# Second cross attention of a two-layer Perceiver block: four PSUM banks for scores, one for the mix, and steps of 3, 3, 3, 2, 2 tiles on TensorE

## What is computed

```
def _L1_xattn_ref(x, context, mask, Wq, Wkv, Wout, b_out):
    HEADS, DIM_HEAD = 16, 64
    q = x @ Wq.T
    k, v = split(context @ Wkv.T, 2, axis=-1)      # 16 heads each
    sim = einsum('bhid,bhjd->bhij', q, k) * DIM_HEAD ** -0.5
    sim = where(mask[:, None, None, :], sim, max_neg)
    attn = softmax(sim, axis=-1)
    out = einsum('bhij,bhjd->bhid', attn, v)       # heads merged
    return out @ Wout.T + b_out
```

## Time and profile before

| | us |
|---|---|
| median of 3 runs | 3442.48 |
| lowest and highest run | 3437.34, 3446.69 |
| the profiled execution, its own time | 3440.26 |
| its span in the profile | 3438.4 |
| this stage's tiles, start of the first mix to the last scores | about 1358 to 2846 |
| engine shares of the whole span: PE, DVE, ACT, POOL | 96%, 69%, 56%, 47% |

### The profile page before, as it was taken

How to read it: one execution, slowest core, us unless ns; L and a number is a source line. 1 busy time by engine, 2 the same in 40 slices (tenths; PEclk the granted TensorE clock), 3 DMA queues, 4 the chain that set the end, 5 groups by cost and what they waited for, 6 DMA issues and landing times. The chain is left out here.

```text
span 3438.4 us, 67642 instructions
## 1 busy us (share of the span) xinstructions
PE 3296.8 (96%) x26448; PEld 1900.8 (55%) x26448; DVE 2386.0 (69%) x5437; ACT 1908.8 (56%) x2600; POOL 1611.6 (47%) x1271
## 2 busy tenths in 40 slices
PE   7799999999998998999999999999999998989999
PEld 4566666666655674545544555555554544655555
DVE  7877877877874436777777777777777775653333
ACT  5466666666664234666666666666666663432222
POOL 5433334333322104777777777777777764310000
PEclk7899999999998899999999999999999999989999
DMA  2133333333310002101111011110111001000000
GB/s 75 32 73 78 79 83 74 77 77 77 79 40 1 26 1 74 39 20 39 39 39 39 20 39 39 39 36 23 39 39 39 26 23 50 1 28 4 4 3 4
DMA packets 90541, 138.92 MB, mean 40 GB/s; under 512 B 14512, under 2 KB 67824, under 8 KB 89456
## 3 DMA queue, kind: packets, MB, share of 16 engines
q1 hardware_dynamic: 90224, 134.61, 14.5%
HBM read 94.15 MB, written 1.05 MB: 28 GB/s over the span
## 5 line engine op out<-in xcount | busy, mean ns | idle before, releaser
L2459 ACT ACTIVATE arena<-banks,arena 128x512 f32<-128x512 f32 x832 | 560.5, 687 | 476.6 <-PE banks L2248 476.6
L2273 PE MATMUL banks<-arena 128*128 128x512 f32 x1664 | 803.9, 603 | 0.8 <-ACT arena L2466 0.8
L2207 POOL TENSOR_TENSOR arena<-arena 128x1024 f32<-128x1024 f32 x256 | 604.3, 2360 | 165.5 <-ACT arena L2466 164.3
L1222 DVE TENSOR_REDUCE arena<-banks 128x1 f32<-128x512 f32 (+1 forms) x896 | 529.7, 628 | 155.1 <-PE banks L1055 150.4
L2361 DVE TENSOR_TENSOR banks<-arena,banks 128x512 f32<-128x512 f32 x640 | 444.6, 695 | 242.2 <-ACT arena L2459 222.8
L1359 ACT ACTIVATE arena<-banks 128x1024 f32<-128x1024 f32 (+1 forms) x448 | 424.0, 962 | 272.2 <-PE banks L1136 272.0
L2378 DVE TENSOR_TENSOR arena<-arena,banks 128x1024 f32<-128x1024 f32 (+1 forms) x448 | 507.5, 1134 | 1.6 <-PE banks L2263 1.2
L2466 ACT ACTIVATE arena<-arena 128x1024 f32<-128x1024 f32 (+1 forms) x448 | 443.0, 989 | 11.1 <-DVE arena L2378 10.9
L2273 PEld LDWEIGHTS banks<-arena 128*128 128x128 f32 x1664 | 289.9, 190 | 220.8 <-issue 200.1
L2247 PE MATMUL banks<-arena 128*128 128x512 bf16 x832 | 315.3, 379 | 0.0
L2246 PE MATMUL banks<-arena 128*128 128x512 bf16 x832 | 314.9, 379 | 0.0
(11 more groups left out here) (353 smaller groups left out, 5167.9 us busy)
## 6 DMA issues: line engine op xcount, KB each, us to landing
arena<-arena SPq DMA_DIRECT2D x768, 50.0 KB, 2.2
arena<-in_ctxT SPq DMA_DIRECT2D x32, 800.5 KB, 6.2
arena<-in_ctx SPq DMA_DIRECT2D x32, 768.0 KB
fold<-in_ctxT SPq DMA_DIRECT2D x16, 800.5 KB, 4.6
foldv<-in_ctxT SPq DMA_DIRECT2D x16, 800.5 KB, 4.7
arena<-in_m2w SPq DMA_DIRECT2D x3, 2048.0 KB, 7.9
arena<-in_xw SPq DMA_DIRECT2D x1, 2048.0 KB, 7.9
weights<-in_weights SPq DMA_DIRECT2D x1, 1920.0 KB, 12.2
```

The lines of the kernel that those rows point to most:

```text
L1222: eng.tensor_reduce(o, s, AX, ALU.max).then_inc(a_max, 1)
L2207: eng.tensor_tensor(part, part, tiles, ALU.add).then_inc(sums, 1)
L2273: eng.matmul(c.ps[:, R_MIX + v % 2, :], ctxn[:, b, kt * D:(kt + 1) * D], st[:, v % 2, kt, :], start=kt == 0, stop=kt == KT - 1).then_inc(m ...
L2459: eng.activation(st[:, v % 2, kt, :], c.ps[:, n % SB, :], ACT.Identity, bias=hide[:, kt, v // 2:v // 2 + 1])\
```

## The change

All of it is in `cross_attention_1`. SB becomes 4, so that scores use banks 0 to 3; the banks of the running maximum and of the shift move up by one, and the mix has one bank, 6, in place of two. With one bank, the first mix of unit v waits for `copy_mix(v - 1)` (before: for `copy_mix(v - 2)`). ScalarE issues `copy_mix` ahead of the score copy of kt 0 and no longer behind it. TensorE takes a unit's tiles in five steps of 3, 3, 3, 2 and 2. `between`, and the kt at which each of its entries stands, is unchanged, and so are VectorE's and POOL's programs.

```
-    SB = 3
+    SB = 4
...
-    R_MAX, R_SHIFT, R_MIX, R_SMALL = 3, 4, 5, 7
+    R_MAX, R_SHIFT, R_MIX, R_SMALL = 4, 5, 6, 7
...
             if kt == 0:
                 eng.wait_ge(ctx_loaded[b], (v // 4 + 1) * 32)
-                wait_if(eng, u_made, v - 1)
+                wait_if(eng, u_made, v)
             eng.wait_ge(exps, v * NP + kt // 2 + 1)
-            eng.matmul(c.ps[:, R_MIX + v % 2, :], ctxn[:, b, kt * D:(kt + 1) * D], st[:, v % 2, kt, :],
+            eng.matmul(c.ps[:, R_MIX, :], ctxn[:, b, kt * D:(kt + 1) * D], st[:, v % 2, kt, :],
...
+        steps = [(0, 3), (3, 6), (6, 9), (9, 11), (11, KT)]
         for v in range(UNITS + 1):
-            for j, a, z in tile_pairs:
+            for a, z in steps:
                 tiles = range(v * KT + a, v * KT + z)
...
         def copy_mix(v):
             eng.wait_ge(mixed, (v + 1) * KT)
             wait_if(eng, y_ps, v - 1)
-            eng.activation(u[:, v % 2, :], c.ps[:, R_MIX + v % 2, :], ACT.Copy).then_inc(u_made, 1)
+            eng.activation(u[:, v % 2, :], c.ps[:, R_MIX, :], ACT.Copy).then_inc(u_made, 1)
...
         for n in range(TILES + KT):
             v, kt = n // KT, n % KT
+            if kt == 0 and v > 0:
+                copy_mix(v - 1)
             if n + LEAD < TILES:
                 copy(n + LEAD)
-            if kt == 0 and v > 0:
-                copy_mix(v - 1)
```

More of the change, by code:

```diff
@@ L2303, in final @@
             mm.then_inc(f_ps, 1)
-        stir(c, eng, R_MIX + 1, 14)
+        stir(c, eng, R_MIX, 14)
         eng.wait_ge(hidden, 3)
@@ L2313, in pe @@
             queries(0, x)
-            stir(c, eng, R_MIX + 1, 5)
+            stir(c, eng, R_MIX, 5)
         eng.wait_ge(unit_made, 1)
@@ L2318, in pe @@
             if n == KT + 1:
-                stir(c, eng, R_MIX + 1, 8)
+                stir(c, eng, R_MIX, 8)
                 turn_peaks(0)
         spread_shift(0)
-        stir(c, eng, R_MIX + 1, 10)
+        stir(c, eng, R_MIX, 10)
         def between(n):
```

## The result

The changed kernel takes 3667.07 us (median of 4 runs, 3663.60 to 3674.64) against 3439.91 for the kernel before beside it (4 runs). The ratio is 1.0658, with a 95% interval of 1.0640 to 1.0677. The direction was right. The size was not: the forecast was 3568, with a range that ended at 3603, and 99 us of the 227 us lost were not in it. The profiled execution of after took 3663.60, its span is 3661.7.

The account below looks back on a forecast made before the run. The prediction took TensorE's instruction stream to bound the stage. It added 104 us (projection and turning) and 22 us (query and final) to the profiled 3440.26, giving 3566, or 3568 as a median, with its own range 3558 to 3600.

Parts of the forecast that it names:

- What bounds the kernel: In this stage TensorE is busy throughout, so the time is its instructions' cost, start to start; the change can only add waits.
- Four score banks and fewer steps: On TensorE's scores: a fourth bank removes no wait, and leaving out four score-mix swaps a unit saves zero.
- One mix bank: A unit's first mix waits for the previous unit's copy_mix, with 1.9 us of cover; costed at nothing.
- Projection and turning: Neighbours on bank 7, so the turning waits for VectorE's four steps: 1.68 us more in 61 units, 1.57 in unit 62, 104 us.
- Query and `final`: In units with v % 4 = 2, final directly follows the kt 11 query and waits for q_low: 15 times 1.49, 22 us.
- Does it spread?: After the turning's stall: VectorE needs about 2.6 us before the shift's spread, TensorE has 4.5 us of work; no second wait.
- The range: Forecast's own range 3558 to 3600; 3548 to 3603 takes in the bounds and the mix bank's case, leaving out some 0.15.
- ready work: Rival: TensorE lets mixes past the waiting turning and final, so both stalls go and the time is 3442; chance 0.03.
- swaps were worth nothing: Rival judged: the four f32-bf16 swaps a unit that go were dear, at 0.6 us each giving 3415; chance 0.02.
- The fallen clock: Rival: TensorE, standing 1.8 us in 25, is granted a clock of 0.97, costing 49 us more, 3617; chance 0.06.
- The rule on order: On TensorE weight loads may be pulled ahead but matmuls stay in program order, so the turning's whole stall is lost.

Follow-up runs that it names:

- the banks alone: The changed kernel with TensorE's seven steps back, keeping four score banks, one mix bank and the earlier copy_mix: 3443.01 us, ratio 1.0010 to the kernel before.
- the steps alone: The kernel before with only the five steps of 3, 3, 3, 2, 2, three score banks and two mix banks kept: 3674.90 us, ratio 1.0680.
- the spread moved: The changed kernel with TensorE's spread_shift at kt 9 instead of kt 8: 3562.70 us, ratio 1.0358 to the kernel before.
- a second bank: The changed kernel with its fourth score bank given to the shift, so the spread waits for shifts two units back: 3561.80 us, ratio 1.0337.
- the kernel with idle times of 2.34 us: The kernel before, steps of two, with TensorE's spread_shift at kt 7 instead of kt 8: 3650.74 us, ratio 1.0598.
- the projection by the turning: The kernel before, steps of two, with TensorE's projection at kt 4 instead of kt 3: 3533.22 us, ratio 1.0260.

## Why the prediction was wrong

- **What bounds the kernel**: right. TensorE's instructions did not change in cost; the base unit grew from 22.82 to 26.25 by waits alone.
- **Four score banks and fewer steps at zero**: right, by the banks alone (3443.01), the steps alone with three banks, and equal periods of 95.24 and 95.22 in steps of three and of two.
- **One mix bank at zero**: right. There is no row for it, and the banks alone cost nothing measurable.
- **Projection and turning, 104 us**: right. The stall was 1.80 as worked out. Moving the turning away gave 110 back, 1.76 a unit in the period (103.75 to 96.72): the 1.80 and the further 0.06 of the turning, less 0.10 by which mixes are slower behind the projection. In unit 62, where the scores have run out, the stall was 3.10 us, 1.57 more than the 1.53 of before, as forecast.
- **Query and `final`, 22 us**: right. 15 waits of 1.41; parting them gave 27 (3452.27 to 3425.66), a figure with the error of two medians, and 1.48 a time in the period (96.72 to 95.24), against 1.49.
- **The step that failed** is the sentence "Does it spread?", which ends in "no second wait". It looked at the spread's wait for the halves of the maxima alone, found 4.5 us of cover for 2.6, and stopped. `spread_shift` has a second wait in its next line, `wait_if(eng, shifted, v * NP)`, for the last shift of the unit in hand. In steps of two the spread came a step after the scores that the maxima ahead of that shift wait for; in steps of three, (6, 9) holds both. Measured: 61 waits, 103.3 us in the row, 1.85 a unit start to start, which is 113 us. By the medians it is 104 with the spread moved and 105 with a second bank, and 112 from the steps alone (3674.90) to the spread moved (3562.70), which ran on one chip; the stages ahead vary from execution to execution (the first score starts anywhere from 1325.96 to 1346.75 in the traces here). With this term the sum is 3568 + 61 x 1.85 = 3681 before what is saved elsewhere. After the turning the mixes start cleanly (2106.73 to the next scores in 2.58, where the mixes behind the projection took 0.10 more than 4 x 0.43 in the earlier trace rows), 6 us over the units, which leaves 3675 against 3667. Of the rest, 2.6 are the median of before, 3442.48 when the sum was made and 3439.91 beside the changed kernel. Within the 61 units the terms close: 61 x (1.68 + 1.85 - 0.10) + 15 x 1.49 = 232 against the 231 measured.
- The forecast's test for it was at hand. The trace of before has one wait of L2262 for L2378, 0.6 us, where the stage begins (the first row, from 1358 to 1375); and in the middle of the stage the last shift ended only 0.66 ahead of the spread, at 2019.67:

```profile
PE banks L2262 <- DVE arena L2378: 0.6, 1, 0.6
...
2018.99 0.68 DVE L2378 TENSOR_TENSOR arena<-arena,banks 128x512 f32<-128x512 f32 x1
...
2020.33 0.22 PE L2262 MATMUL banks<-arena 128*128 128x128 bf16 x1
```

Both say that the two are close neighbours in time, and the price stood there too. The spread starts 0.15 after that shift ends (2112.96 to 2113.11 above), so 0.51 of the 0.66 was to spare. Steps of three take two mixes and a tile of scores, 2.37 us, from between the maxima's scores and the spread. That makes an estimate of 2.37 - 0.51 = 1.86 of stall, against 1.85 measured.
- **The range** took its width from the terms that were known. A term that had been left out could not be in it. The chances given to what lies outside it, 0.03, 0.02 and 0.06, add up to 0.11 and not to some 0.15.
- **The rivals**: ready work did not fill the stalls, and swaps were worth nothing. The fallen clock did not come while scores last: the 61 units have a granted clock of 1.00. It came behind them, after the 3.03 us of idle time in unit 62, where the three mixes that follow take 5.01 us and not 2.58:

```profile
3075.11 1.11 PE L2254 MATMUL banks<-consts,arena 128*128 128x128 f32 x4 [3.03 <-DVE arena L2399]
3076.02 5.17 PE L2273 MATMUL banks<-arena 128*128 128x512 f32 x6
3081.03 0.22 PE L2262 MATMUL banks<-arena 128*128 128x128 bf16 x1
```

In the kernel with idle times of 2.34 us it came again and again.
- **The rule on order** that the prediction takes from the Trainium skill stands on the page it names, TensorE: Matmul & The Clock Gate, but in the section "Step-by-step: what each phase is for": only weight loads are pulled ahead, matmuls stay in program order. The trace of after agrees: 61 times TensorE stood for 1.7 us or more at the turning, with mixes queued behind it.

## What to carry to other kernels

When work is regrouped, make a list of every wait of every instruction that moves, from the code, and price each by itself. A wait that costs nothing has no row in the trace, and the one that is close to costing is found only by the distance between its release and its waiter. Small products that share a bank, or overwrite what another engine still reads, want a step's worth of other work between them; a spare bank is worth most where it ends such a wait. On a kernel bound by one engine's stream of instructions, larger groups brought nothing here, and the starts had shown beforehand that the swaps between them cost nothing.

## What the runs showed of the hardware

An idle time of TensorE can cost more than itself. While scores last, no idle time of 1.67 to 1.74 us was followed by a lower clock; there are 59 and 61 of them in after (turning and spread), as many in the steps alone, 59 each in the kernels with the spread later and with two shift banks, and 60 with the projection by the turning. Ten idle times were of 2.02 or 2.03, two in each of these five kernels; four were followed by it, with the unit 1.7 us longer, and none of those in after and the steps alone. Of those of 2.34 about half were, and not at random: from 2038 to 2723 us it was the same two neighbours of every four. The 2.44 and 2.45 us at the first spread of the loop, in after and the steps alone, were not; all four of 3.03 or 3.04, in unit 62, were. The busy time by stretch shows two units with the same instructions, both with 2.03 us of idle time at the turning, in the kernel with the spread one step later (the granted clock is the third number from the end):

```profile
1796.10:1821.68 25.58, 23.45 (x109) 12.09 (x110) 18.52 (x29) 15.65 (x23) 17.56 (x12) 1.00 0.02 5
2626.35:2653.63 27.28, 25.15 (x109) 12.68 (x110) 18.52 (x29) 15.66 (x23) 17.57 (x12) 0.94 0.02 5
```

What decides in a given case, beyond the idle time, these runs do not settle. The Trainium skill (TensorE: Matmul & The Clock Gate, "What's actually happening") describes a gate with just two levels, set by how busy the engine has been. The starts here agree: a mix's matmuls stand 0.43 us apart or 0.85.
